# Group statistics of four fused pair layers: the row sums with the data tile as PE's weights and one column of ones moving

## The reference

```python
def _gn(v, G=32, eps=1e-05):
    g = v.reshape(B_, H_, W_, G, C_ // G)
    m = jnp.mean(g, axis=(1, 2, 4), keepdims=True)
    s = jnp.var(g, axis=(1, 2, 4), keepdims=True)
    return ((g - m) / jnp.sqrt(s + eps)).reshape(v.shape)
```

## Time and profile before

| | us |
|---|---|
| median of 3 runs | 1818.19 |
| lowest, highest | 1813.92, 1819.84 |
| the profiled execution | 1815.44 |
| its span, first to last instruction | 1813.7 |
| PE, PEld busy in the span | 1453.9, 982.0 |
| DVE, ACT, POOL busy in the span | 1503.7, 1095.1, 969.2 |

### The profile page before, as it was taken

The page is one execution under the profiler, slowest core; times in us unless marked ns, Lnnn a source line. Parts: engine busy times, 40 slices in busy tenths (PEclk is TensorE's granted clock), DMA queues, the critical chain, the costliest instruction groups (busy, mean ns, idle before and its releaser), DMA issues.

```text
span 1813.7 us, 30465 instructions
## 1 busy us (share of the span) xinstructions
PE 1453.9 (80%) x9712; PEld 982.0 (54%) x9712; DVE 1503.7 (83%) x3826; ACT 1095.1 (60%) x2284; POOL 969.2 (53%) x665
## 2 busy tenths in 40 slices
PE   5569998899779997898899846666666489998765
PEld 1146666765456666765587613333333267767654
DVE  6889993398799992399689989999999699981588
ACT  2246662399646562399543367777777267771598
POOL 7378870187588870287555503333333488850354
PEclk8779999899979999899999958889899889999789
DMA  7024435277634435377544304344444434436377
GB/s 258 0 70 112 109 88 134 82 215 206 172 84 106 108 88 136 84 218 194 173 108 112 79 18 111 94 114 97 113 98 110 117 94 107 115 73 150 120 259 248
DMA packets 408831, 225.51 MB, mean 124 GB/s; under 512 B 343456, under 2 KB 343776, under 8 KB 408672
## 3 DMA queue, kind: packets, MB, share of 16 engines
q1 hardware_dynamic: 270240, 185.81, 37.4%
q10 hardware_dynamic: 138432, 37.76, 8.9%
HBM read 114.97 MB, written 66.06 MB: 100 GB/s over the span
## 4 chain that ended last, share of the span: by engine, by line
issue 32%; PE 31%; DVE 14%; ACT 11%; POOL 8%; DMA 3%; SPq 0%; ACTq 0%; POOLq 0%; DVEq 0%
PE ps L1145 11%; ACT work L992 8%; PE ps L1150 7%; PE ps L1106 5%; POOL work L518 4%; PE ps L1135 4%; PE ps L1225 4%; POOL work L472 3%; DMA gate_dram<-work 2%; DVE work L746 2%; ACT work L978 2%; DVE stats L804 2%; DVE work L634 1%; DVE tok L814 1%; DVE pairs L851 1%
## 5 line engine op out<-in xcount | busy, mean ns | idle before, releaser
L512 POOL TENSOR_TENSOR ln_s<-ln_s,half_power 128x8 f32<-128x8 f32 x216 | 358.7, 1661 | 358.9 <-DVE ln_s L728 306.1
L1106 PE MATMUL ps<-work,ones 128*128 128x512 f32 x504 | 281.6, 676 | 58.2 <-ACT work L954 48.4
L1145 PE MATMUL ps<-work 128*128 128x384 f32 x864 | 318.7, 492 | 2.1 <-ACT work L978 2.1
L1003 ACT ACTIVATE work<-ps 128x768 f32<-128x768 f32 x216 | 175.2, 811 | 170.3 <-DMA gate_dram<-work 128.2
L992 ACT ACTIVATE work<-pairs,ln_s 128x64 f32<-128x64 f32 x648 | 264.0, 502 | 19.1 <-DVE ln_s L735 19.1
L1150 PE MATMUL ps<-work 128*128 128x256 f32 x864 | 223.8, 382 | 0.0
L518 POOL TENSOR_TENSOR work<-pairs,work 128x512 f32<-128x512 f32 x36 | 75.9, 2108 | 273.6 <-DVE pairs L914 273.6
L1150 PEld LDWEIGHTS ps<-work 128*128 128x128 f32 x864 | 165.8, 192 | 69.8 <-issue 1.8
L1145 PEld LDWEIGHTS ps<-work 128*128 128x128 f32 x864 | 157.3, 192 | 67.2 <-ACT work L978 3.5
L746 DVE TENSOR_SCALAR work<-work,ln_s 128x64 f32<-128x64 f32 x468 | 189.9, 474 | 0.0
L1135 PE MATMUL ps<-ident,work 128*128 128x128 f32 x864 | 142.9, 291 | 53.8 <-DVE work L746 42.5
(11 more groups left out here) (149 smaller groups left out, 2805.5 us busy)
## 6 DMA issues: line engine op xcount, KB each, us to landing
work<-x_mid SPq DMA_DIRECT2D x144, 256.0 KB, 2.8
gate_dram<-work ACTq DMA_DIRECT2D x108, 256.0 KB, 3.1
work<-gate_dram SPq DMA_DIRECT2D x108, 256.0 KB, 3.1
work<-in_x_in SPq DMA_DIRECT2D x72, 256.0 KB, 2.8
work<-x_nat SPq DMA_DIRECT2D x144, 128.0 KB, 3.0
x_mid<-work SPq DMA_DIRECT2D x72, 256.0 KB, 2.6
work<-pairs SPq DMA_DIRECT2D x96, 96.0 KB, 3.0
work<-pairs ACTq DMA_DIRECT2D x96, 96.0 KB, 3.2
```

Of the source, the lines that this page charges most:

```text
L512: pool.tensor_tensor(ln_s[:, b, RSTD, :], ln_s[:, b, VAR, :], half_power[:, 0:U], ALU.pow)\
L1003: act.activation(sig[:, b, :].rearrange("p (k g) -> p k g", k=PAIRS)[:, 2 * half:2 * half + 2, :], ps[:, bank:bank + 2, 0:GATES], ACT.Sigm ...
L1106: last = pe.matmul(ps[:, bank, :], ones[:], src[:, b, :], start=first, stop=end, skip_group_check=True)
L1145: last = pe.matmul(ps[:, GATE_BANK[half] + k, 0:GATES], xnT[:, b, (2 * half + k) * P:(2 * half + k + 1) * P], wpair[:, VALUES:VALUES + GAT ...
```

## The change

For layers 1 to 3 the operands change places. The tile is now PE's weights, 128 of its columns at a time, and one column of ones moves. A product of that kind sums over the rows as before, but its result is one column, in which partition p holds the sum of column p of the 128 (one of two tokens' 64 channels). `PAIRS` is 4, so each bank takes 4 products a tile and holds 4 columns. After the last tile DVE adds the 4 columns of each bank (`gn_by_row`), multiplies them with `of_group`, which holds a one where partition p belongs to group g, and PE sums over the rows with a product with ones of 64 columns into bank 1; DVE copies that into `gn_s`. The sums of the input keep the old form. `of_group` is made at the start on DVE from the identity; the unused `ident16` goes away with its two POOL operations.

```diff
-            pool.memset(ident16[:], 0.0).then_inc(s_const, 1)
...
-            pool.wait_ge(s_const, 7)
-            for m in (ident, ident16):
+            pool.wait_ge(s_const, 6)
+            for m in (ident,):
...
             dve.wait_ge(anchor_sum, 1)
+            dve.tensor_reduce(of_group[:], ident[:].rearrange("p (u g e) -> p g u e", u=2, e=2), AX.XY, ALU.add)
...
-                dve.tensor_reduce(gn_s[:, 0, :], ps[:, SUM, :].rearrange("p (u g e) -> p g u e", u=U, e=2), AX.XY, ALU.add)
-                step(dve.tensor_reduce(gn_s[:, 1, :], ps[:, SQ, :].rearrange("p (u g e) -> p g u e", u=U, e=2), AX.XY, ALU.add), 1)
+                if l == 0:
+                    dve.tensor_reduce(gn_s[:, 0, :], ps[:, SUM, :].rearrange("p (u g e) -> p g u e", u=U, e=2), AX.XY, ALU.add)
+                    step(dve.tensor_reduce(gn_s[:, 1, :], ps[:, SQ, :].rearrange("p (u g e) -> p g u e", u=U, e=2), AX.XY, ALU.add), 1)
+                else:
+                    dve.tensor_reduce(gn_by_row[:], ps[:, SUM:SQ + 1, 0:PAIRS], AX.X, ALU.add).then_inc(gn_row_step, 1)
+                    dve.wait_ge(gn_row_step, 3 * l - 2)
+                    for k in range(2):
+                        dve.tensor_scalar(gn_rows[:, k, :], of_group[:], gn_by_row[:, k:k + 1], None, ALU.mult).then_inc(gn_row_step, 1)
+                    dve.wait_ge(gn_collected, l)
+                    step(dve.tensor_copy(gn_s[:, 0:2, :], ps[:, 1, 0:2 * GROUPS].rearrange("p (k g) -> p k g", k=2)), 1)
...
-            pe.wait_ge(s_const, 9)
+            pe.wait_ge(s_const, 7)
...
+            def square_sums_of_input(t, b):
+                pe.wait_ge(sq_ready, t + 1)
+                pe.matmul(ps[:, SQ, :], ones[:], squares[:, b, :], start=t == 0, stop=t == TILES - 1, skip_group_check=True)\
+                    .then_inc(sums_ready, 1)
+
             def add_to_sums(t, r, b, which=(SUM, SQ)):
 
                 pe.wait_ge(sq_ready, r + 1)
-                first = isinstance(t, int) and t == 0
-                end = isinstance(t, int) and t == TILES - 1
                 for bank in which:
                     src = shifted if bank == SUM else squares
-                    last = pe.matmul(ps[:, bank, :], ones[:], src[:, b, :], start=first, stop=end, skip_group_check=True)
+                    for k in range(PAIRS):
+                        last = pe.matmul(ps[:, bank, k:k + 1], src[:, b, k * P:(k + 1) * P], ones[:, 0:1],
+                                         start=t == 0 and k == 0, stop=t == TILES - 1, skip_group_check=True)
...
             for l in range(layers):
+                if l:
+                    pe.wait_ge(gn_row_step, 3 * l)
+                    pe.matmul(ps[:, 1, 0:2 * GROUPS], ones[:], gn_rows[:].rearrange("p k g -> p (k g)"), start=True, stop=True)\
+                        .then_inc(gn_collected, 1)
                 pe.wait_ge(gn_picked, l + 1)
```

More of the change, by code:

```diff
@@ L166, in build @@
         ident = sb("ident", [P, P])
-        ident16 = sb("ident16", [P, P], BF16)
         ones = sb("ones", [P, P])
@@ L191, in build @@
         gn_s = sb("gn_s", [P, 8, GROUPS])
+        of_group = sb("of_group", [P, GROUPS])
+        gn_by_row = sb("gn_by_row", [P, 2])
+        gn_rows = sb("gn_rows", [P, 2, GROUPS])
         gn_roots = sb("gn_roots", [P, GROUPS])
@@ L246, in build @@
          mlp_out_ready, mres_loaded,
-         s_apart) = [sem(f"sem_{k}") for k in range(81)]
+         gn_row_step, gn_collected,
+         s_apart) = [sem(f"sem_{k}") for k in range(83)]
         x_loaded, gate_stored, xnew_stored, mres_loaded, qT_ready, hqT_ready = [
@@ L1111, in _ @@
             for k, (lo, hi) in enumerate(SUM_PARTS):
-                pipeline(pe, [(0, lambda t, b: add_to_sums(t, t, b, (SQ,)))], hi - lo, lo)
+                pipeline(pe, [(0, square_sums_of_input)], hi - lo, lo)
                 if 1 <= k <= 3:
```

## The result

The changed kernel takes 1859.72 us (median of 4 runs, 1855.76 to 1869.19) against 1818.74 us before (now four runs): a ratio of 1.0238, interval 1.0194 to 1.0282, so 2.4% slower. (The ratio is worked out from all runs; the two medians alone give 1.0225.) The profiled execution took 1855.76 us, its span is 1853.6 us.

A forecast was written before the change was run, and what follows sets the result against it. It took ACT, DVE and PE as nearly full together in the output stages, DVE in layer 2's second loop; 2.0 + 0.6 + 0.2 + 20 + 3 = 26 us gave 1841 for the profiled execution, 1844 us as median; range 1815 to 1895.

The forecast's parts named there:

- The sums at high clock: Output stages of layers 0 and 1: 16 loads take 1.78 us, 0.06 more than before; +2.0 us over the steady tiles.
- Rival (c): Sums: loads run beside each other at high clock, so sums leave PE; -6.4 us, 1812 us; chance 0.05.
- The statistics: Group statistics, layers 1 to 3: added steps take 1.5 us for 1.33; +0.2 us at each of three places, +0.6.
- The start: Kernel start: reduction of the identity into of_group goes ahead of the anchor on DVE; +0.2 us.
- The clock: Output stages of layers 0 and 1: one-column loads do not lift PE's low clock, 1.2 GHz; +20 us.
- 5.9 us a tile at low clock: Output stages of layers 0 and 1: PE's projection, transposes and sums at low clock, against 3.43 us a tile.
- four such stretches: Two starts and two pauses in output stages 0 and 1: 12 us each at low clock, 42% lost; +20 us.
- The stage ends: Bare last sums at three stage ends: no term in the sum; Rival (c) had them shrinking, 4.4 us gained.
- Layer 2: Second loop: PE needs 9.98 us a tile at low clock against DVE's 10.09; +3 us, bounds 0 and 31.
- 0.9 us a tile in the upper bound: Layer 2's second loop: stalls over 34 tiles if the clock stays low, giving the bound of 31 us.
- Rival (a): Output stages: loads with one-column matmuls count as work, clock behaves as before; +2.8 us, 1821 us; chance 0.32.
- Rival (b): Clock stays low through both output stages: 170 us there and 15 in layer 2, 2006 us; chance 0.12.

The follow-up runs named there:

- e1: Changed kernel with each sum product moving 128 columns of ones instead of 1, same loads; 1820.25 us, ratio 1.0017 to the kernel before.
- e5: Changed kernel with 64 moving columns of ones per sum product instead of 1; 1829.77 us, ratio 1.0083 to the kernel before.
- e6: Changed kernel with 32 moving columns of ones per sum product instead of 1; 1840.29 us, ratio 1.0128 to the kernel before.
- e8: The changed kernel unaltered, measured once more beside the kernel before; 1858.87 us, ratio 1.0242.
- e4: New form of the sums in layer 2 alone, layers 0 and 1 as in the kernel before; 1821.31 us, ratio 1.0022.
- e3: New form of the sums in the output stages of layers 0 and 1 alone, layer 2 as before; 1844.61 us, ratio 1.0154.
- e9: Kernel before, old product, with squares rounded to bf16 and added with bf16 ones; 1809.21 us, ratio 0.9942.
- e11: Changed kernel with shifted tile and squares in bf16, so 8 bf16 loads a tile instead of 16 f32; 1805.63 us, ratio 0.9950.

## Why the prediction was right

The sign, the range (1815 to 1895) and the mechanism held; the size, +26 us, was too small by 14 of the 40 us of span. The same sum, part by part, with what the two traces show (each part is read between the same instructions in both):

| part of the sum | forecast, us | measured, us |
|---|---|---|
| output stages 0 and 1, first to last projection (steady tiles and low stretches) | 2.0 + 20 | 11.4 + 10.3 |
| the same two stages, last projection to DVE's first statistics step | 0 | 3.2 + 3.5 |
| layer 2's loop, to the last addition on POOL | 3 | 3.9 |
| layer 2, from there to DVE's first statistics step | 0 | 1.6 |
| the statistics' own steps, three times | 0.6 | 0.9 |
| the start and all stages without a change | 0.2 | 5.3 |

**The sums at high clock.** Forecast 16 x 0.111 us and +0.06 us per pair of tiles; measured 6.91 for 6.86. Right. e1 and the trace show that the loads take exactly the columns' place. Rival (c) fell with it. The floor of about 25 ns that the Trainium skill gives for matmuls of 1 to 64 columns ("TensorE: Matmul & The Clock Gate", "Back-to-back issue gap") is not reached where each brings a load of 128 f32 columns: these were 0.111 us apart.

**The statistics.** Forecast +0.2 us each, measured +0.3. **The start.** Forecast 0.2 us; the reduction into `of_group` (L567) starts at 5.75 us and the anchor's (L568) at 5.95, 0.20 us after it. Right.

**The clock.** "I take it that loads do not lift it" was the step that decided, and e1, e5 and e6 bear it out: with the same loads, the more columns they move, the less time is spent at low clock. The 5.9 us a tile at low clock was 5.98. "There are four such stretches ... 4 x 12 x 0.42" came out nearly at its time (21.7 us with the steady tiles, for 22), but by luck. The four forecast places were there, but the clock also fell four times while PE was at work (at 410, 451, 806 and 854 us). The stretches with sums were 3 to 18 us long instead of 12. In layer 0 from 371 to 490 us a mean clock of 0.85 means 30% of 119 us at low clock, 36 us, and in layer 1 0.89 from 793 to 912 us means 26; I had 24 us for a stage. Part of that excess was given back at layer 0's pause. The second execution of the same kernel (e8) lost 15.1 and 22.4 us from first to last projection, so +20 is no better than an order of size.

**The stage ends.** This is the term that was mis-sized: the sum has none for the bare sums at the three stage ends, so it puts them at 0. The clock was low there (0.64 from 499 to 510 us, 0.50 from 922 to 931 and from 1465 to 1478; before, 1.00 from 487 to 493). The time from the last projection to DVE grew by 3.2 and 3.5 us, and the last tile's sums of layer 2 took 3.58 us for 1.98. That is 8.3 of the missing 14 us. My own bound for rival (c) had priced these bare sums, in the other direction only.

**Layer 2.** Forecast 9.98 us of PE a tile at low clock and +3 us, with bounds 0 and 31. It was 10.25: each group of 8 loads takes 1.80 us, not 1.68, because the first load after another product's is bare (the load and its product both start at 1255.71). The 0.9 us a tile in the upper bound came from no row; where PE was the bound a tile lost 0.16. The clock was 0.58 on average, so the cover was gone in part of the loop, as forecast, and e4 shows it alone.

**Rival (a)**, the clock as before, is refuted: without the streaming it isn't, with it (e1) it is. **Rival (b)**, a clock that stays low, did not come in the output stages: each stretch ended, with only projections and transposes streaming. In layer 2's loop the clock did stay low for long, 290 us in e4 (1170 to 1460 us at 0.50), where it costs little. Of the rule on transposes in the Trainium skill ("TensorE: Matmul & The Clock Gate", "Part 4: PE-mode transpose") no run here is a test, as none takes the transposes alone.

The 5.3 us in stages that the change doesn't touch are not explained. The input stage of layer 0 (first projection to first product) took 177.2 us before, 178.3 after and 176.8 in e1. All the rest together lies between 1147.4 us (e3) and 1156.2 (e9) in the traces of the experiments, and was 1148.0 in the second execution of the changed kernel, so a difference of 5 us between two executions says nothing of the change.

## What to carry to other kernels

Exchanging the operands of a product to move one column instead of 512 saves nothing where each product then needs its own f32 weight load: count loads and columns together, at both clock levels. Before taking streaming away from PE, ask what else keeps its clock up and whether PE still fits at half speed; if neither, the columns are worth keeping even when they compute the same number 128 times (e1). The sums were better made cheaper by precision than by shape: bf16 operands in the old form gave 1.3%, where the values can bear the rounding. And look at each stage's end: work that is covered in the steady part stands bare there, at whatever clock it meets.

## What the runs showed of the hardware

A kernel that does 128 times the multiplications in its sums, with the same instructions, was 2.2% faster (e1 against e8: ratio 1.0017 against 1.0242). The granted clock fell to 1.2 GHz while PE went without a pause from transposes into loads with one column each (410 us; PE busy 7.00 of the next 7 us, clock 0.51). Being busy did not bring it back at once: from 371 to 389 us PE was busy 18.00 of 18 us at 0.50. Between one column and 128 the loss was graded, not a switch. A chain of f32 loads of 128 columns ran at 0.111 us from start to start at high clock and 0.213 at low, with 1 (L1122 of the changed kernel) or with 128 columns moving (e1). Eight bf16 loads with one column each took 0.38 us at low clock (381.13 in e11) and 0.35 at high (399.21).
